# Order of z's pair-sum product and the next group's conv1 in the last chunk of the gates, in a fused GNN layer with GRU gates

## What is computed

```python
h     = relu(bn1(conv1d(xT, conv1_w)))            # width 1
x_conv= relu(bn2(conv1d(h, conv2_w, pad 8)) + xT) # width 17
s     = x @ w_se.T + b_se                         # 3 numbers per node
A     = exp(-dist(s, s)) * adj
msg   = relu(x @ w_msg.T + b_msg)
x_nmp = A @ msg                                   # the "pair sums" below
gi    = concat(x_conv, x_nmp) @ w_ih.T + b_ih     # parts r, z, n
gh    = x @ w_hh.T + b_hh                         # parts r, z, n
r, z  = sigmoid(gi_r + gh_r), sigmoid(gi_z + gh_z)
n     = tanh(gi_n + r * gh_n)
out   = layernorm(x + (1 - z) * n + z * x)
```

## Time and profile before

| | |
|---|---|
| median of 3 runs | 298.09 us (297.8 to 299.0) |
| the profiled execution | 298.04 us |
| its span, first to last instruction | 295.8 us |
| time outside the span | 2.2 us |
| mean granted TensorE clock | 0.994 |
| TensorE matmul busy | 286.9 us, 97% of the span |
| VectorE busy | 246.5 us, 83% |
| ScalarE busy | 200.5 us, 68% |
| GpSimd busy | 45.0 us, 15% |
| share of the chain that ended last on TensorE | 90% |

### The profile page before, as it was taken

The page is one execution under the profiler, slowest core; times in us unless marked ns, Lnnn a source line. Parts: engine busy times, 40 slices in busy tenths (PEclk is TensorE's granted clock), DMA queues, the critical chain, the costliest instruction groups (busy, mean ns, idle before and its releaser), DMA issues.

```text
span 295.8 us, 5038 instructions
## 1 busy us (share of the span) xinstructions
PE 286.9 (97%) x1500; PEld 238.0 (80%) x1500; DVE 246.5 (83%) x690; ACT 200.5 (68%) x464; POOL 45.0 (15%) x79
## 2 busy tenths in 40 slices
PE   8999999999999999999999999999999999999992
PEld 6787788888877888888878888988878798888881
DVE  2799899889989988659998997749998997935795
ACT  2889656688874769478774769568884777724444
POOL 3000004300103060001101251001100324000113
PEclk9999999999999999999999999999999999999997
DMA  7502451461013122812213031642200031330002
GB/s 243 228 2 72 143 175 40 119 236 47 28 37 109 71 96 86 243 76 71 71 35 106 6 136 71 198 157 71 71 35 35 0 141 71 86 127 0 6 32 106
DMA packets 12257, 27.23 MB, mean 92 GB/s; under 512 B 1363, under 2 KB 2133, under 8 KB 12117
## 3 DMA queue, kind: packets, MB, share of 16 engines
q1 hardware_dynamic: 11956, 26.03, 26.4%
q10 hardware_dynamic: 288, 1.05, 1.1%
HBM read 22.88 MB, written 4.19 MB: 92 GB/s over the span
## 4 chain that ended last, share of the span: by engine, by line
PE 90%; DVE 5%; ACT 2%; issue 1%; POOL 1%; POOLq 0%; DVEq 0%; ACTq 0%
PE bank L379 87%; PE bank L650 2%; DVE first L1397 1%; DVE x_lo L1239 1%; PE bank L432 1%; ACT x_hi L747 1%; DVE xr L1613 0%; DVE xr L1618 0%; ACT hn L988 0%; ACT bank L769 0%; DVE first L1403 0%; POOL first L1074 0%; ACT msg L759 0%; DVE xn L1410 0%; POOLq L85 0%
## 5 line engine op out<-in xcount | busy, mean ns | idle before, releaser
L379 PE MATMUL bank<-x_hi,w_hl 128*128 128x512 f32 (+1 forms) x122 | 44.7, 407 | 1.0 <-DVE x_lo L1239 1.0
L379 PE MATMUL bank<-ec_hi,w_hl 128*128 128x512 f32 (+1 forms) x98 | 35.7, 391 | 0.0
L379 PEld LDWEIGHTS bank<-x_hi,w_hl 128*128 128x128 f32 x122 | 23.0, 188 | 6.8 <-DVE x_lo L1239 2.4
L1125 POOL TENSOR_TENSOR EF<-EF 128x132 f32<-128x132 f32 x12 | 6.5, 539 | 137.2 <-DVE EF L1299 137.2
L863 ACT ACTIVATE xn<-xn,first 128x128 f32<-128x128 f32 x48 | 19.1, 485 | 7.3 <-DVE first L1417 7.3
L379 PE MATMUL bank<-T_hi,cw_hi 128*128 128x256 f32 (+1 forms) x71 | 24.0, 338 | 0.0
L379 PE MATMUL bank<-x_lo,w_hl 128*128 128x512 f32 (+1 forms) x61 | 23.7, 388 | 0.0
L379 PE MATMUL bank<-ec_hi,cw_hi 128*128 128x512 f32 x56 | 23.2, 413 | 0.1
L379 PE MATMUL bank<-ec_lo,cw_hi 128*128 128x512 f32 x56 | 22.4, 400 | 0.0
L379 PE MATMUL bank<-ec_hi,cw_lo 128*128 128x512 f32 x56 | 22.3, 399 | 0.0
L379 PE MATMUL bank<-T_hi,cw_lo 128*128 128x256 f32 (+1 forms) x71 | 22.1, 312 | 0.0
(11 more groups left out here) (183 smaller groups left out, 834.0 us busy)
## 6 DMA issues: line engine op xcount, KB each, us to landing
adj<-adj_dram SPq DMA_DIRECT2D x16, 512.0 KB, 5.0
x<-xt_dram SPq DMA_DIRECT2D x16, 256.0 KB, 3.2
xn<-xn_dram SPq DMA_DIRECT2D x16, 256.0 KB, 4.9
out_dram<-xn SPq DMA_DIRECT2D x15, 256.0 KB, 2.1
xr<-xt_dram SPq DMA_DIRECT2D x12, 256.0 KB, 3.8
xn<-wcv_dram SPq DMA_DIRECT2D x1, 1024.0 KB, 7.6
xr<-xt_dram ACTq DMA_DIRECT2D x1, 768.0 KB, 5.9
EF<-wsm_dram SPq DMA_DIRECT2D x1, 512.0 KB, 3.2
```

The costliest lines, as they stand in the source:

```text
L379: return nc.tensor.matmul(out, lhs, rhs, start=start, stop=stop, skip_group_check=True)
L1125: nc.gpsimd.tensor_tensor(next_diff(k), even[:, :, 2:], odd[:, :, 0:HQ - 2], ALU.subtract).then_inc(odd_step, 1)
```

## The change

In the last chunk's gates, where a next group follows, z's part on the pair sums (IMZ, three matmuls) is issued ahead of the next group's conv1 of chunk 3, and no longer behind it. In the other chunks, and in the last group, the two lines stand in the same order as before, since conv1 isn't issued at that place there.

```diff
                 if k >= 1:
                     part(r_bank, ICR, ck, stop=True).then_inc(rhn_done, 1)
+                part(z_bank, IMZ, mk)
                 if k == NC - 1 and not last:
                     conv1(g + 1, k)
-                part(z_bank, IMZ, mk)
                 if k >= 1:
                     pe.wait_ge(narg_ready, 4 * g + k)
                 part(in_bank, IMN, mk, start=True)
```

## The result

The changed kernel took 296.14 us (median of 6 runs, 295.84 to 297.55) against 298.12 us for the kernel before (6 runs, 297.80 to 299.00). The ratio is 0.9933, with a 95% interval of 0.9912 to 0.9954. The forecast was 296.3 us, in a range of 295.7 to 297.4.

The account below looks back on a forecast made before the run. TensorE's instructions and gaps were taken as the bound. Closing three gaps, 1.865 us, less 0.06 for weight loads gave 1.80 us off 298.04, or 296.24; forecast 296.3 us, range 295.7 to 297.4.

Parts of the forecast that it names:

- The bound: Whole kernel: TensorE's instructions and the gaps between them set the time, with matmuls filling 97% of the span.
- The gap's price: TensorE in front of conv1: passages between groups lose 0.615, 0.625 and 0.625 us, 1.865 us in all.
- conv1's place: TensorE behind IMZ: conv1 moves three matmuls back to 82.66, its release stays at 82.47, leaving 0.19 us in hand.
- The weight load: conv1's load behind the `x_lo` wait: up to 0.04 us late, priced at 0.02 us a passage, 0.06 in all.
- What takes conv1's result: ScalarE and VectorE: relu starts at about 83.57 at no cost; L1606 loses 0.54 us idle, L1391 keeps 0.37.
- Everything behind slides as one piece: All engines behind the passage: gates, transposes, messages, residual and conv2 move earlier together by 0.6 us.
- Rival A: VectorE at L1606 has no reserve, a late relu gives back 0.3 us a passage: 297.2 us, chance 0.10.
- Rival B: Behind the passage or at conv1, another wait leaves an equal TensorE gap: about 298.1 us, chance 0.08.
- Rival C: conv1 held behind IMZ with the gap at full size, conv2 0.24 us later each passage: 298.8 us, chance 0.05.

Follow-up runs that it names:

- the repeat: The changed kernel measured again beside the other runs on one chip, against the kernel before: 296.37 us, ratio 0.9938.

## Why the prediction was right

**The bound.** TensorE's order and gaps set the time: over the runs the ratio rises with the passage, from 0.9933 at 68.41 us to 1.0041 at 69.46 us, except for passages less than 0.1 us apart, which the times don't tell apart.

**The gap's price.** I took 1.865 us from two steps around the gap, not the 1.0 us that the wait itself was given. The passages and the last stretch give 1.87 us. The run with `x_lo` 0.35 us later confirms that this gap followed `x_lo`.

**conv1's place.** 82.66 in the old trace is 0.93 us behind ICR's last matmul; it is 82.33 - 81.40 = 0.93 us. relu was to come at about 83.57, 1.84 us behind it, and came at 83.23, 1.83 us behind it.

**The weight load.** This term of the sum was mis-sized. The load does start 0.04 us behind the matmul ahead, as I said, but I allowed 0.06 us in all, and no cost shows: some 0.12 us are free. The other side of this is that conv1 had less in hand than the 0.19 us that I read from the matmuls: what counts is the weight load, and for that the reserve is 0.12 - 0.04 = 0.08 us. With 0.19 us in hand, the run with 0.35 us of delay would have cost 0.16 us a passage; it cost 0.25. The forecast didn't depend on this, because `x_lo` kept its time.

**What takes conv1's result.** L1606 lost all its idle time and nothing else, and L1391 kept 0.38 us (0.37 forecast).

**"Everything behind slides as one piece."** True, but I didn't see how much hung on it. I had looked at the waits that the profile lists, and the chain from z's last product over both other engines to `third` is in none of them, since it is only 0.07 us late. Because ICZ slid with the rest, the chain slid too. That this place held was luck as far as my account goes, since I hadn't looked at it. In the run with the transposes ahead of ICZ, where z's last product comes 0.43 us later, 0.45 of the 0.63 us went.

**The rivals.** Rival A's mechanism is real, but I priced it too high. With IMZ and IMN both ahead, the relu starts 0.75 us later than in the kernel before, of which A covers 0.46 us and gives back 0.29; 0.19 us came back. I had counted the reserve before L1391 from the end of L1606's record of 0.69 us, and L1391 can start 0.60 us behind its start, which makes the cover 0.09 us larger. C's 0.46 us has the same fault. The change itself doesn't reach A. Rival B did not occur: no new wait stands on TensorE, and the three passages each kept their gain. Rival C did not occur: conv1 was taken up when due. A slower kernel by the path that A and C name exists: with conv1 behind ICN, the residual is late and conv2 waits for it.

**The time.** 296.14 us against 296.3. The medians lie 1.98 us apart, 0.11 us more than the 1.87 us of the gaps, which is within the scatter; in the repeat they lie 1.80 us apart (298.17 and 296.37). The span was to be about 294.0 us and was 293.6; the difference is the 0.33 us ahead of the first passage, which the repeat doesn't show. So how close a single pair of medians comes to the forecast is in part luck, and the passages are the better witness.

## What to carry to other kernels

A gap in front of a waiting instruction, on the engine that is the bound, can be filled by independent work that stands behind it (two different products did it equally here), and its price is read from the distance of starts around it (0.61 to 0.63 us here), not from the wait's own figure (0.34 us). How far the waiting instruction may move back is set by the queue of the engine that takes its result: here the first three matmuls were free, the next three (0.70 us) cost 0.19 us, and then it was one for one. Before the next reordering look for places where the bound engine runs a little late without a listed wait; here one such place, 0.07 us late, marked a chain with no reserve.

## What the runs showed of the hardware

For matmuls of 128x512 in this kernel, at a granted clock of 1.00:

- A weight load behind an open semaphore wait stays behind it, even where nothing else is loaded (idle for 0.42 us in the run with `x_lo` 0.35 us later), though the wait is for the other operand.
- A load 0.04 us behind the start of the matmul ahead of it cost nothing. One 0.17 us behind cost 0.06 us, and one 0.38 us behind (82.68 against 82.30) cost 0.25 us. All three fit the estimate that some 0.12 us are free, and in the two late ones the second matmul follows the load by 0.34 to 0.35 us.
- With the load 0.17 us late the record of its own matmul doesn't move; only the distance to the next one does, 0.28 us instead of 0.23.
